# A macaron layer: first pass and attention in one block, with the last parts of q and k made in another order and on other engines

## What is computed

```
x = x + 0.5 * ffn(layernorm(x))
x = x + attention(layernorm(x))
x = x + 0.5 * ffn(layernorm(x))
```

```
q, k, v = split(x @ W_attn + b_attn);   s = q @ k^T
s = s - s.mean(-1);   s = s / (abs(s).mean(-1) + 1e-6) * score_gain;   s = where(causal, s, -1000)
r = max(s, 0) ** 4;   att = r / (r.sum(-1) + 1e-6);   y = (att @ v) @ W_proj + b_proj
```

## Time and profile before

| | |
|---|---|
| runs | 465.9, 467.62, 469.6 us; median 467.62 |
| profiled execution | 466.43 us, of which the span of its instructions 464.5 |
| busy in the span | PE 408.8 (88%), DVE 380.6 (82%), ACT 340.6 (73%), POOL 292.8 (63%) |
| granted clock, mean | 0.978 |
| end of the first block | about 110.6 us from the start of the span |
| last fourth power on POOL | 370.3 |

### The profile page before, as it was taken

How to read it: one execution, slowest core, us unless ns; L and a number is a source line. 1 busy time by engine, 2 the same in 40 slices (tenths; PEclk the granted TensorE clock), 3 DMA queues, 4 the chain that set the end, 5 groups by cost and what they waited for, 6 DMA issues and landing times.

```text
span 464.5 us, 13512 instructions
## 1 busy us (share of the span) xinstructions
PE 408.8 (88%) x5034; PEld 189.8 (41%) x5040; DVE 380.6 (82%) x929; ACT 340.6 (73%) x609; POOL 292.8 (63%) x214
## 2 busy tenths in 40 slices
PE   2998889854899999899999999999999978999895
PEld 1333334431344444444444444444444444434342
DVE  5766565657999999999999999999999976846643
ACT  3653255834999999999999999999999724463321
POOL 3004932515989999999999999999999940020000
PEclk9999999985999999999999999999999997999999
DMA  8000001353705106114033051061003100000001
GB/s 201 9 0 1 1 1 46 95 99 102 137 5 89 41 1 105 26 31 79 19 62 67 3 98 31 3 103 25 3 9 83 38 11 0 1 1 23 23 0 47
DMA packets 18239, 19.97 MB, mean 43 GB/s; under 512 B 4904, under 2 KB 10632, under 8 KB 18184
## 3 DMA queue, kind: packets, MB, share of 16 engines
q1 hardware_dynamic: 17896, 19.18, 19.7%
q10 hardware_dynamic: 288, 0.01, 0.0%
HBM read 13.02 MB, written 6.03 MB: 41 GB/s over the span
## 4 chain that ended last, share of the span: by engine, by line
PE 35%; ACT 18%; DVE 12%; issue 10%; ACTq 1%; DVEq 0%
PE bank L1207 14%; PE bank L1244 10%; ACT bank L1340 8%; ACT arena L1350 6%; DVE arena L1310 4%; PE bank L1608 3%; PE bank L1574 3%; PE bank L1578 2%; DVE bank L1316 2%; DVE arena L1846 1%; ACT arena L1329 1%; PE bank L1514 1%; ACT arena L1354 1%; DVE arena L1853 1%; PE bank L1586 0%
## 5 line engine op out<-in xcount | busy, mean ns | idle before, releaser
L1376 POOL TENSOR_TENSOR arena<-arena 128x1024 f32<-128x1024 f32 (+1 forms) x144 | 241.0, 1706 | 17.4 <-ACT arena L1350 16.7
L1310 DVE SCALAR_TENSOR_TENSOR arena<-bank,masks 128x512 f32<-128x512 f32 x288 | 180.7, 691 | 4.3 <-PE bank L1207 4.3
L1350 ACT ACTIVATE arena<-arena 128x1024 f32<-128x1024 f32 (+1 forms) x160 | 147.8, 958 | 0.8 <-DVE arena L1310 0.2
L1207 PE MATMUL bank<-Q,K 128*32 128x512 bf16 (+3 forms) x1536 | 97.2, 332 | 21.4 <-PEq L1068 9.2
L1340 ACT ACTIVATE bank<-bank 128x1024 f32<-128x1024 f32 (+5 forms) x144 | 90.0, 625 | 6.7 <-PE bank L1207 6.2
L1207 PE MATMUL bank<-K,Q 128*32 128x512 bf16 (+3 forms) x1536 | 93.8, 330 | 0.0
L1316 DVE TENSOR_SCALAR_CACHE_REDUCE bank<-bank 128x896 f32<-128x896 f32 (+4 forms) x112 | 84.7, 789 | 0.0
L1244 PE MATMUL bank<-arena,Vq 128*32 128x512 f32 (+3 forms) x768 | 77.0, 486 | 0.0
L1207 PEld LDWEIGHTS bank<-Q,K 128*32 128x32 bf16 x1536 | 37.5, 96 | 87.7 <-issue 31.8
L1244 PE MATMUL bank<-arena,ones_rows 128*32 128x512 f32 (+3 forms) x640 | 59.4, 464 | 0.0
L1207 PEld LDWEIGHTS bank<-K,Q 128*32 128x32 bf16 x1536 | 40.1, 97 | 29.0 <-DVE arena L1310 6.2
(11 more groups left out here) (188 smaller groups left out, 477.8 us busy)
## 6 DMA issues: line engine op xcount, KB each, us to landing
Q<-q_parts SPq DMA_DIRECT2D x21, 192.0 KB
K<-k_parts SPq DMA_DIRECT2D x14, 128.0 KB
att<-arena SPq DMA_DIRECT2D x28, 64.0 KB, 1.6
q_parts<-arena SPq DMA_DIRECT2D x6, 256.0 KB, 2.9
k_parts<-arena SPq DMA_DIRECT2D x6, 256.0 KB, 2.9
K<-k_parts SPq DMA_DIRECT2D x7, 192.0 KB
K<-k_parts SPq DMA_DIRECT2D x18, 64.0 KB
X<-in_L_attn_x SPq DMA_DIRECT2D x4, 256.0 KB, 4.4
```

What stands on the lines that cost most here:

```text
L1207: last = nc.tensor.matmul(m.bank[j:j + 32, at + lo:at + hi], left[par][:, g, blk * P + j:blk * P + j + 32], right[par][:, g, s0:s0 + hi - ...
L1310: nc.vector.scalar_tensor_tensor(Y(r, g)[:, y0:y0 + SPAN], m.bank[:, at:at + SPAN], 0.0, mask, ALU.max, ALU.mult).then_inc(relu_done, 1)
L1350: nc.scalar.activation(z, Y(r, g)[:, tile_low(r) - off(r):T - off(r)], ACT.Square)\
L1376: nc.gpsimd.tensor_tensor(z, z, z, ALU.mult).then_inc(fourth_p, 1)
```

## The change

1. `first_pass` and `attention` become one function, `layer`, with one block. Each engine runs its part of the first pass and goes on with its part of attention. In place of the block's end stand waits: PE waits for the constants, for `x_added`, for all 26 of `silu_ready` before its first fill, and for all 26 of `prod_ready` before the first upper tile; DVE and ACT wait for the constants; POOL for `prod_ready`. In quad 0, ACT waits for the rests before round 1's squares, for the low parts before round 2's, and also for `v_out` before round 3's.
2. In the list of items ("v", 1) stands before ("qk", 3). An item's halves can be issued apart (`gate_half`, `up_half`): PE issues v of span 2 ahead of the transposes of span 3, then q of span 3, v of span 3, k of span 3.
3. For batch 1, k's rest, middle and low parts are made by POOL, after q's rest and low part and after the addition for v. The middle part is a `tensor_copy` on POOL. ACT makes q's high and middle and k's high part. DVE ends with the centring of k.
4. The three operations of `Finish.slope` move from the start of attention on DVE to chunk 9 of the first pass.

```diff
-        self.items = ffn(0, 17) + [("qk", 0), ("qk", 1)] + ffn(17, 20) + [("v", 0), ("qk", 2), ("qk", 3), ("v", 1)]
+        self.items = ffn(0, 17) + [("qk", 0), ("qk", 1)] + ffn(17, 20) + [("v", 0), ("qk", 2), ("v", 1), ("qk", 3)]
...
         item(23)
-        pe.wait_ge(project.norm.xnT_ready, 3)
+        gate_half(24)
         project.transpose(pe, 3, self.attention_xt_ps[3])
-        item(24)
-        item(25)
+        gate_half(25)
+        up_half(24)
+        up_half(25)
...
         norm_last_tile(nc, m, project.norm, act, 3)
+        item(24)
         project.take(act, 3, self.attention_xt_ps[3])
-        item(24)
-        act.wait_ge(self.silu_ready, 25)
+        item(25)
+        act.wait_ge(self.silu_ready, 26)
         project.high_part(act, "q", 1)
+        project.middle_part(act, "q", 1)
         act.wait_ge(project.k_centred, 2)
         project.high_part(act, "k", 1)
-        item(25)
-        project.middle_part(act, "q", 1)
-        project.middle_part(act, "k", 1)
...
         project.v_full(minus, 0, project.v_raw).then_inc(project.v_out, 1)
+        pool.wait_ge(self.silu_ready, 25)
+        project.v_full(minus, 2, project.v_raw).then_inc(project.v_out, 1)
         project.rest_part(pool, minus, "q", 1)
         project.low_part(pool, minus, "q", 1)
-        pool.wait_ge(self.silu_ready, 26)
-        project.v_full(minus, 2, project.v_raw).then_inc(project.v_out, 1)
+        project.rest_part(pool, minus, "k", 1)
+        pool.wait_ge(project.rest_ready["k"], B)
+        nc.gpsimd.tensor_copy(project.of(project.parts["k"][1], 1), project.of(project.rest["k"], 1))\
+            .then_inc(project.middle["k"], 1)
+        project.low_part(pool, minus, "k", 1)
...
                 project.signs(dve, link)
+                finish.slope(dve)
...
         item(24)
-        dve.wait_ge(self.prod_ready, 25)
+        item(25)
+        dve.wait_ge(self.prod_ready, 26)
         project.centre_k(link, 1)
-        item(25)
-        project.rest_part(dve, nc.vector.tensor_tensor, "k", 1)
-        project.low_part(dve, nc.vector.tensor_tensor, "k", 1)
...
+                        if first_quad(q) and (r, g, kind) == (0, 0, "upper"):
+                            pe.wait_ge(first.prod_ready, len(first.items))
...
+            first.tensor(pe)
+            pe.wait_ge(m.attention_made, ATTENTION_MADE)
+            pe.wait_ge(first.x_added, NSPAN)
+            pe.wait_ge(first.silu_ready, len(first.items))
...
-            finish.slope(dve)
+            first.vector(dve, finish)
+            dve.wait_ge(m.attention_made, ATTENTION_MADE)
...
+                    elif (r, g) == (1, 0):
+                        act.wait_ge(project.rest_ready["q"], B)
+                        act.wait_ge(project.rest_ready["k"], B)
+                    elif (r, g) == (2, 0):
+                        act.wait_ge(project.low["q"], B)
+                        act.wait_ge(project.low["k"], B)
                     elif (r, g) == (NR - 2, 0):
+                        act.wait_ge(project.v_out, B)
                         act.wait_ge(m.parts_stored, 16 * 4 * PARTS)
...
+            first.scalar(act)
+            act.wait_ge(m.attention_made, ATTENTION_MADE)
...
+            first.gpsimd(pool)
+            pool.wait_ge(first.prod_ready, len(first.items))
             copy_v(0)
```

More of the change, by code:

```diff
@@ L197, in build @@
         m.down_loaded, m.attention_loaded = sem("down_weights_loaded"), sem("attention_weights_loaded")
-        m.operands_zeroed = sem("operands_zeroed")
+        m.operands_zeroed, m.attention_made = sem("operands_zeroed"), sem("attention_constants")
         m.parts_stored = sem("parts_stored")
@@ L205, in build @@
         weights = (w_attn, b_attn, w_proj, b_proj, score_gain, w_gate, w_up, w_down, sw_gate, sw_up, sw_down)
-        first_pass(nc, m, sem, First(nc, m, sem, start, f1_norm, project), lambda sp: load_weights(m, sp, *weights))
-        attention(nc, m, sem, q_dram, k_dram, att_dram, project, out)
+        first = First(nc, m, sem, start, f1_norm, project)
+        layer(nc, m, sem, first, lambda sp: load_weights(m, sp, *weights), q_dram, k_dram, att_dram, out)
 NORM_WORDS = NT * (C + 3)
@@ L302, in moments, with attention_constants @@
         span_moments(self.nc, self.m, dve, i, self.stats_ready).then_inc(norm.moments_ready, 1)
-def attention_constants(nc, m, sem, pool):
-    zeroed, made = m.operands_zeroed, sem("attention_constants")
+def attention_constants(nc, m, pool):
+    zeroed, made = m.operands_zeroed, m.attention_made
     for t in (*m.Q, *m.K):
@@ L346, in attention_constants @@
         link(nc.gpsimd.memset(m.den[B - 1][n * HB:n * HB + N_HEAD, :], 0.0))
+ATTENTION_MADE = 4 + 2 + 1 + QUARTERS
 def span_stats(nc, m, i, stats_ready):
@@ L677, in turn_weights, with gate_half @@
                 last.then_inc(self.wt_ready, 1)
-        def item(r):
+        def gate_half(r):
             kind, n = self.items[r]
-            gate, up = self.gate_ps[r % 2], self.up_ps[r % 2]
+            gate = self.gate_ps[r % 2]
             if kind == "ffn":
@@ L692, in item @@
                 pe.wait_ge(project.norm.xnT_ready, n + 1)
+            else:
+                pe.wait_ge(project.norm.xnT_ready, 2 * n + 1)
             if r >= 2:
@@ L695, in item, with up_half @@
             if kind == "ffn":
-                first = nc.tensor.matmul(gate, m.WG[:, c * P:(c + 1) * P], x, start=True, stop=True)
+                last = nc.tensor.matmul(gate, m.WG[:, c * P:(c + 1) * P], x, start=True, stop=True)
             elif kind == "qk":
-                first = project.rows("q", n, gate)
+                last = project.rows("q", n, gate)
             else:
-                first = project.values(2 * n, gate)
-            first.then_inc(self.gate_ready, 1)
+                last = project.values(2 * n, gate)
+            last.then_inc(self.gate_ready, 1)
+        def up_half(r):
+            kind, n = self.items[r]
+            up = self.up_ps[r % 2]
             if r >= 2:
@@ L704, in item @@
             if kind == "ffn":
-                second = nc.tensor.matmul(up, m.WU[:, c * P:(c + 1) * P], x, start=True, stop=True)
+                i, c = self.span_of(n), self.chunk_of(n)
+                last = nc.tensor.matmul(up, m.WU[:, c * P:(c + 1) * P], m.xnT[:, i * SPAN:(i + 1) * SPAN],
+                                        start=True, stop=True)
             elif kind == "qk":
-                second = project.rows("k", n, up)
+                last = project.rows("k", n, up)
             else:
-                second = project.values(2 * n + 1, up)
-            second.then_inc(self.up_ready, 1)
+                pe.wait_ge(project.norm.xnT_ready, 2 * n + 2)
+                last = project.values(2 * n + 1, up)
+            last.then_inc(self.up_ready, 1)
+        def item(r):
+            gate_half(r)
+            up_half(r)
         def spread_weights(n):
@@ L894, in scalar, with gpsimd @@
         norm_last_tile(nc, m, project.norm, act, 3)
+        item(24)
         project.take(act, 3, self.attention_xt_ps[3])
-        item(24)
-        act.wait_ge(self.silu_ready, 25)
+        item(25)
+        act.wait_ge(self.silu_ready, 26)
         project.high_part(act, "q", 1)
+        project.middle_part(act, "q", 1)
         act.wait_ge(project.k_centred, 2)
         project.high_part(act, "k", 1)
-        item(25)
-        project.middle_part(act, "q", 1)
-        project.middle_part(act, "k", 1)
-    def gpsimd(self, pool, sem):
+    def gpsimd(self, pool):
         nc, project = self.nc, self.project
@@ L910, in gpsimd @@
         pool.wait_ge(self.parts_ready, 2)
-        attention_constants(nc, self.m, sem, pool)
+        attention_constants(nc, self.m, pool)
         minus = nc.gpsimd.tensor_tensor
@@ L917, in gpsimd, with vector @@
         project.v_full(minus, 0, project.v_raw).then_inc(project.v_out, 1)
+        pool.wait_ge(self.silu_ready, 25)
+        project.v_full(minus, 2, project.v_raw).then_inc(project.v_out, 1)
         project.rest_part(pool, minus, "q", 1)
         project.low_part(pool, minus, "q", 1)
-        pool.wait_ge(self.silu_ready, 26)
-        project.v_full(minus, 2, project.v_raw).then_inc(project.v_out, 1)
-    def vector(self, dve):
+        project.rest_part(pool, minus, "k", 1)
[3 more added lines that the diff above has]
+        project.low_part(pool, minus, "k", 1)
+    def vector(self, dve, finish):
         nc, m, s, project = self.nc, self.m, self.norm, self.project
@@ L1058, in vector, with layer @@
         item(24)
-        dve.wait_ge(self.prod_ready, 25)
+        item(25)
+        dve.wait_ge(self.prod_ready, 26)
         project.centre_k(link, 1)
-        item(25)
-        project.rest_part(dve, nc.vector.tensor_tensor, "k", 1)
-        project.low_part(dve, nc.vector.tensor_tensor, "k", 1)
[L1066 to L1092, removed]
+def layer(nc, m, sem, first, load, q_dram, k_dram, att_dram, out):
+    start, project = first.start, first.project
     a = Arena(m)
@@ L1165, in body @@
```

(3 more changed lines are left out.)

## The result

The changed kernel takes 461.21 us (459.61 to 463.24, four runs) where the kernel before takes 467.69: a ratio of 0.9857, with an interval of 0.9826 to 0.9888. That is 6.5 us less, inside the range, 2.2 above the forecast of 459.0. The profiled execution took 461.15 us.

The account below looks back on a forecast made before the run. With all engines full in mid-attention, only attention's ends, here the barrier seam before it, could yield time: 466.43 - 8.0 (9.0 earlier start, POOL stall 1.0) = 458.4, or 459.6 by the runs' median; 459.0 given, range 455.5 to 463.5.

Parts of the forecast that it names:

- The seam is the place, the beat does not change: Gain comes only where the first pass meets attention, at the block's end; quads stay at 32.06 us, every engine being full.
- POOL's chain: Batch 1's q and k parts one after another, then v's copy; POOL starts fourth powers at 110.55, 4.2 us earlier.
- the slower rival: POOL's copy of k's middle to bfloat16 takes a slow path; at 15 us the time is 472.3; chance 0.05.
- DVE and ACT: At attention's start, DVE takes up masks at 102.45, 9.0 us earlier; ACT starts sums at 103.55, 9.1 earlier.
- POOL late by 1.0 before the first power sum: In quad 0 PE stands 1.0 us for round 0's fourth powers, ending at 118.0, so the gain is 8.0, not 9.0.
- The rival that the stall is made good: POOL catches up in quad 0, DVE and ACT keep their 9.0 us: 457.4 us; chance 0.12.
- The rival that POOL stays late: POOL holds PE again in rounds 1, 2 and 3 by about 1 us each: 461.4 us; chance 0.13.
- The seam not won through the port: DVE's masks stand beside POOL's parts until k's low part ends at 110.1; gain only 1.3: 465.1 us; chance 0.10.
- The slope, ACT's waits, SP's queue: Slope in chunk 9, ACT's waits in quad 0 and SP's stores and loads cost nothing; slope at most 0.7 us without cover.
- PE's clock and v in the gap: v of span 2 fills PE's 1.67 us gap before span 3's transposes; clock stays 2.4 GHz, q reaches ACT at 97.35.
- the 1.01 us: Amount by which q of span 3 and everything after it come later if PE's clock falls as before.
- The sum: Profiled execution 466.43 less the gain of 8.0 is 458.4 us; 459.6 by the median of runs; 459.0 given.

Follow-up runs that it names:

- the second execution: The changed kernel profiled once more with no edit: 461.12 us, ratio 0.9861 to the kernel before, seam 70.25 us.
- the run with POOL later: Changed kernel plus a POOL memset of 2048 columns ahead of the copy of v for quad 0: 463.85 us, ratio 0.9913.
- v last: Changed kernel with ("qk", 3) before ("v", 1) again and POOL's addition for v between q's rest and low part: 461.61 us, ratio 0.9864.
- one block alone: Kernel before with one block and the slope in chunk 9, its items, engines and order of parts kept: 464.74 us, ratio 0.9930.
- the second execution of before: The kernel before, unedited, run again for its trace alone: seam 76.82 us, no time given.

## Why the prediction was right, and where it was off

- *The seam is the place, the beat does not change.* Right: quad to quad 31.96 us, and the 7.9 us gained at the mark in quad 1 are gained ahead of attention's second quad.
- *POOL's chain.* Right nearly step by step. Behind the transposes the working has the first fourth power at 110.55 - 90.64 = 19.9 us; it came at 111.87 - 91.78 = 20.1. The first power sum was forecast 27.4 us behind them and came at 27.6. The copy to bfloat16, taken at 1.1 from memsets, took 1.04; the slow path, the slower rival, was not taken.
- *DVE and ACT.* Forecast 11.8 and 12.9 us behind the transposes, measured 103.81 - 91.78 = 12.0 and 104.89 - 91.78 = 13.1. The reason for DVE's start was the working's own, POOL's rest of q, only in the second execution (first mask 11.75 behind the transposes). In the profiled one DVE waited for k, which the half clock made late.
- *POOL late by 1.0 before the first power sum.* It was 1.34, and the run with POOL later shows that what is added to it counts nearly in full (1.75 of 1.81). The rival that the stall is made good fell with that. The rival that POOL stays late fell as it was put (three more stalls): once PE is held, everything behind it shifts along. But what lies behind it is true: POOL's whole work up to round 2 of quad 0 is the limit.
- *The seam not won through the port.* Fell: four masks take 2.48 us beside POOL's parts, as four did in the kernel before beside POOL's fourth powers.
- *The slope, ACT's waits, SP's queue.* Nothing of them is seen in the waits.
- *PE's clock and v in the gap.* This is the step that failed. I put the half clock near 97 us down to the gap and counted on v to remove it. The gap stands in four executions (both of before, v last, one block alone), and the clock fell behind it in one, the profiled one of before. With v in the gap it fell in four of nine, near 98.5 us, when most of q was made: q came to ACT 7.72 us behind the transposes in that execution of before, and 6.8 to 7.1 in the twelve others. The size was short as well: the 1.01 us were read from q alone, but k was held up too, and the seam was 1.49 us longer (78.31 and 76.82). Between executions with the clock at 1.00 in the stretch of span 3 the gain is 76.82 - 70.25 = 6.6 us. That the profiled pair shows 7.9 for the 8.0 forecast is luck: the execution of before that I reckoned from had the half clock where it cost 1.5 us, the changed one where it cost 0.2 (70.45 and 70.25).
- *The sum.* It gives 458.4 from the profiled execution, and the profiled execution after took 461.15, 2.7 more. Of this 0.1 is the seam, 1.14 were lost ahead of it, and 1.02 behind it: from the mark to the end of the span 458.8 - 162.23 = 296.57, before 464.5 - 168.95 = 295.55. These two are the scatter of executions, since the thirteen traces have 90.64 to 93.12 us ahead of the transposes and 295.2 to 298.0 behind the mark. The last 0.42 lie outside the span: 461.15 - 458.8 = 2.35, where the sum kept the 1.93 of before (466.43 - 464.5). They are not scatter (2.2 to 2.4 us in every execution of the changed kernel, 1.8 to 2.1 in every one of before), and no run shows their cause. The ends of the range were added up wrongly by 0.2 and 0.1: their terms give 455.7 and 463.6.

## What to carry to other kernels

When a barrier goes, work out for each engine when it can start, and then ask which engine's whole amount of work up to the first meeting is largest: reordering within that engine mostly moved its stall here, while an operation of 0.40 us moved into time in which it waited gained 0.3. Work may be given to the slower engine if the one that is relieved would otherwise start later: k's parts took longer on POOL and still gained 4 us. Before a stretch at low clock is made a term of the sum, look whether another execution has it.

## What was not expected of the hardware

The stretches with a granted clock of 0.50 differ from execution to execution of one kernel. Near 13 us the first matmuls of the first ffn took about twice as long as later ones, for longer in the changed kernel's profile. Before, the second item's pair of 512-column matmuls:

```profile
15.59 1.12 PE L696 MATMUL bank<-xnT,WG 128*128 128x512 f32 x2
16.55 1.02 PE L705 MATMUL bank<-xnT,WU 128*128 128x512 f32 x2
```

After, the first item's pair, the first half of the second item (1.14 us later than before), and the granted clock over the same stretch:

```profile
12.68 2.08 PE L701 MATMUL bank<-xnT,WG 128*128 128x512 f32 x2
14.55 1.86 PE L715 MATMUL bank<-xnT,WU 128*128 128x512 f32 x2
...
16.73 1.12 PE L701 MATMUL bank<-xnT,WG 128*128 128x512 f32 x2
```

```profile
12.00:16.00 4.00, 4.00 (x6) 1.18 (x4) 1.71 (x8) 3.96 (x6) 0.00 (x0) 1.00 0.12 28
```

Two matmuls take 1.02 us at 16.55 and 1.86 at 14.55, and the granted clock is shown as 1.00 for both. At 96.28, where it is shown as 0.50, two took 3.44 / 2 = 1.7 us. The durations near 13 us are those of the half clock, then, though the profile does not show one there. Why is open.

A DVE operation of 0.75 us on 1024 columns in SBUF (L551) took 2.58 in the second execution of before: it began at 101.76, 0.1 us after POOL began the rest of q, and ended at 104.34, 0.55 us after that had ended. The Trainium skill says so (SBUF — State Buffer, section Who interferes with whom: DVE in a two-port mode and GpSimd lock each other out for a whole instruction), and the trace agrees with 2.58 against 0.75; the mode itself it does not show. Where the first addition of the centring was the one to meet POOL, that one took 1.89 in place of 0.16 us. POOL can be the one held up: with k's parts back on DVE, its copy of v, 0.40 us otherwise, took 1.40 from 106.13 on, beside DVE's rest of k (105.02 to 107.27).
